# Padding that moves the buffers of the scores and of the first MLP layer, and other unread products around the kernel's work

## The reference, cut to what matters

```
mod = (silu(c) @ wmod)                       # six vectors of 256 per batch: sa, ca, ga, sb, cb, gb
ga, gb = signs kept, magnitudes at least 0.25
h = layernorm(x) * (1 + ca) + sa
scores = (h * w_lhs) @ (h * w_rhs).T          # 1024 x 1024 per batch
x = x + ga * softmax(scores) @ h
h = layernorm(x) * (1 + cb) + sb
x = x + gb * (relu(h @ W1 + b1) @ W2 + b2)    # W1: 256 x 1024, W2: 1024 x 256
```

## The kernel before, in words

| buffer | role | before | mod 512 | changed | mod 512 |
|---|---|---|---|---|---|
| W1hi, W1lo | F stationary | 17024, 25216 | 128 | the same | 128 |
| W2hi, W2lo | G moving | 33408, 41600 | 128 | the same | 128 |
| Phi, Plo | AV stationary | 87104, 99392 | 64 | the same | 64 |
| Lhi, Llo | SC stationary | 111680, 119872 | 64 | the same | 64 |
| Rhi, Rlo | SC moving | 128064, 136256 | 64 | 128512, 136704 | 0 |
| V | AV moving | 144448 | 64 | 144960 | 64 |
| hid_hi, hid_lo | G stationary | 198336, 204480 | 192 | 198848, 204992 | 192 |
| h2hi, h2lo | F moving | 210624, 218816 | 192 | 211520, 219712 | 64 |

## Time and profile before

### The profile page before, as it was taken

How to read it: one execution, slowest core, us unless ns; L and a number is a source line. 1 busy time by engine, 2 the same in 40 slices (tenths; PEclk the granted TensorE clock), 3 DMA queues, 4 the chain that set the end, 5 groups by cost and what they waited for, 6 DMA issues and landing times.

```text
span 691.5 us, 13488 instructions
## 1 busy us (share of the span) xinstructions
PE 686.1 (99%) x4621; PEld 627.7 (91%) x4621; DVE 558.4 (81%) x1059; ACT 427.5 (62%) x625; POOL 361.7 (52%) x396
## 2 busy tenths in 40 slices
PE   9999999999999999999999999999999999999998
PEld 8688899998999989998999989999899998999997
DVE  5699989799898898978989799887989887876421
ACT  3265398736786367683786647864678634845562
POOL 3572576636654386352872458643665434523644
PEclk9999999999999999999999999999999999999999
DMA  8211761137431382315622266112843126003300
GB/s 294 81 49 59 204 193 55 39 107 252 123 100 56 103 232 91 99 61 179 180 67 90 67 226 185 61 38 98 258 121 99 46 91 221 1 1 100 100 31 30
DMA packets 61663, 77.54 MB, mean 112 GB/s; under 512 B 5632, under 2 KB 54336, under 8 KB 61632
## 3 DMA queue, kind: packets, MB, share of 16 engines
q1 hardware_dynamic: 61632, 77.14, 35.5%
HBM read 46.15 MB, written 30.97 MB: 112 GB/s over the span
## 4 chain that ended last, share of the span: by engine, by line
PE 94%; DVE 4%; issue 0%; ACT 0%; DMA 0%; DVEq 0%; ACTq 0%; SPq 0%
PE col L595 9%; PE col L594 9%; PE col L593 9%; PE acc L530 8%; PE acc L531 8%; PE acc L536 8%; PE score L694 8%; PE score L690 8%; PE score L691 8%; PE score L578 4%; PE score L579 4%; PE score L580 4%; PE score L576 2%; PE score L584 2%; PE score L499 1%; DVE S L879 1%
## 5 line engine op out<-in xcount | busy, mean ns | idle before, releaser
L1088 POOL TENSOR_TENSOR hid_lo<-hid,hid_hi 128x512 fp32r<-128x512 f32 x127 | 175.4, 1386 | 143.2 <-ACT hid_hi L719 142.8
L715 ACT ACTIVATE hid<-col,b1T 128x512 f32<-128x512 f32 x128 | 87.0, 679 | 140.3 <-PE col L595 126.1
L530 PE MATMUL acc<-W2hi,hid_hi 128*128 128x256 f32 x480 | 119.2, 282 | 0.0
L531 PE MATMUL acc<-W2lo,hid_hi 128*128 128x256 f32 x480 | 116.9, 278 | 0.0
L690 PE MATMUL score<-V,Phi 128*128 128x258 f32 x448 | 108.8, 281 | 0.0
L691 PE MATMUL score<-V,Phi 128*128 128x256 f32 x448 | 108.6, 281 | 0.0
L719 ACT ACTIVATE hid_hi<-hid 128x512 fp32r<-128x512 f32 x128 | 81.0, 633 | 37.6 <-PE acc L536 29.8
L593 PE MATMUL col<-h2hi,W1hi 128*128 128x512 f32 x256 | 102.4, 400 | 0.0
L595 PE MATMUL col<-h2hi,W1lo 128*128 128x512 f32 x256 | 101.0, 395 | 0.0
L594 PE MATMUL col<-h2lo,W1hi 128*128 128x512 f32 x256 | 100.6, 393 | 0.0
L530 PEld LDWEIGHTS acc<-W2hi,hid_hi 128*128 128x128 f32 x480 | 90.4, 188 | 2.1
(11 more groups left out here) (139 smaller groups left out, 1493.2 us busy)
## 6 DMA issues: line engine op xcount, KB each, us to landing
block_rows<-blocks SPq DMA_DIRECT2D x29, 512.0 KB, 2.9
blocks<-block_rows SPq DMA_DIRECT2D x116, 128.0 KB, 3.0
x_cur<-x SPq DMA_DIRECT2D x16, 512.0 KB, 3.9
ln_t<-x SPq DMA_DIRECT2D x14, 512.0 KB, 4.8
score_blocks<-stage SPq DMA_DIRECT2D x14, 512.0 KB, 4.2
lower<-score_blocks SPq DMA_DIRECT2D x56, 128.0 KB, 2.9
out<-x_mlp SPq DMA_DIRECT2D x8, 512.0 KB, 3.0
out<-x_mlp SPq DMA_DIRECT2D x15, 256.0 KB, 2.2
```

The costliest lines, as they stand in the source:

```text
L530: nc.tensor.matmul(o, hi, W2hi[:, it, :], start=(it == 0 and (apart or t % 2 == 0)), stop=False, skip_group_check=True)
L531: nc.tensor.matmul(o, hi, W2lo[:, it, :], start=False, stop=False, skip_group_check=True)
L715: nc.scalar.activation(hid[:, n % 2, :], col[n % 2][:], ACT.Relu, bias=b1T[:, n % FT:n % FT + 1]).then_inc(col_read, 1)
L1088: G.tensor_tensor(hid_lo[:, n % RING, :], hid[:, n % 2, :], hid_hi[:, n % RING, :].bitcast(F32), ALU.subtract).then_inc(hid_lo_done, 1)
```

## The change

```diff
         Lhi, Llo = sb("Lhi", [P, DK, ROWS], F32R), sb("Llo", [P, DK, ROWS], F32R)
+        sb("before_R", [P, 112])
         Rhi, Rlo = sb("Rhi", [P, DK, ROWS], F32R), sb("Rlo", [P, DK, ROWS], F32R)
+        sb("behind_R", [P, 16])
...
         hid_hi, hid_lo = sb("hid_hi", [P, RING, HR], F32R), sb("hid_lo", [P, RING, HR], F32R)
+        sb("before_h2", [P, 96])
         h2hi, h2lo = sb("h2hi", [P, DK, ROWS], F32R), sb("h2lo", [P, DK, ROWS], F32R)
...
+            def keep_busy_split(moving, stationary, count):
+
+                for _ in range(count):
+                    nc.tensor.matmul(col[0][:, 0:moving.shape[-1]], stationary, moving, start=True, stop=True)
...
                             last.then_inc(tile_done, 1)
+
+                        for at in (120, 96, 32):
+                            keep_busy_split(h2hi[:, 0, 0:HR], W1hi[:, 0, at:at + P], 5)
                     elif kind == "MA":
                         pe.wait_ge(pool_const, 2)
-                        keep_busy(20)
+                        keep_busy(10)
+                        pe.wait_ge(const_ready, 3)
+
+                        keep_busy_split(h2hi[:, 0, 0:1].broadcast_to([P, HR]), h2hi[:, 0, HR:HR + P], 5)
+                        keep_busy_split(h2hi[:, 0, 0:HR], h2hi[:, 0, HR + 32:HR + 32 + P], 5)
                         pe.wait_ge(silu_step, 1)
...
             V_.memset(V_first[:, :, D + 1:VW], 0.0).then_inc(const_ready, 1)
+            V_.memset(h2hi[:, 0, :].bitcast(F32), 0.0).then_inc(const_ready, 1)
```

## The result

The changed kernel takes 695.49 us (median of 8 runs, 694.61 to 695.78), the kernel before 693.53 us on the same chip (8 runs). The ratio is 1.0024, with a 95% interval of 1.0015 to 1.0033: slower, by little more than such a measurement resolves. The forecast was 688.2 us.

A forecast was written before the change was run, and what follows sets the result against it. TensorE was taken as the bound, with products in flight 686.1 of 691.5 us. Savings 4.0 + 2.1 + 1.2 - 1.0 = 6.3, less 0.4 and the end's 0.3, gave 5.6 us: 693.8 to 688.2, range 686.8 to 692.0.

The forecast's parts named there:

- Is 64 as good at 512 columns? One place says so: Last score product ahead of F, at distance 64, lasts 388 ns against its line's mean of 391; taken as evidence for 64.
- a floor for every distance, 388: Shortest duration in ns of 512-column products, used to price F and the wide scores at distance 64.
- F at 448 with 388 and 394 in turn: Warning in the prediction: behind G, F at distance 448 lasts 388 ns on line 593 but 394 on line 595.
- 398 behind AV: Warning in the prediction: F on line 593 lasts 398 ns behind AV, so delay depends on what went before.
- the third, slower: Rival: at 512 columns 64 leads into the 398 ns step everywhere; F +3.8 us, wide scores +1.3, 697.9 us; chance 0.08.
- a weight load that ends halfway: Slower rival's reason: at 512 columns the weight load, about as long as 256 columns, ends halfway; chance 0.08.
- F at 64: F's 768 products, lines 593 to 595, at 388 ns each apart from start-ups: 4.0 us saved.
- Scores: Score products moved to distance 64: 0.8 us saved at 512 columns, 1.0 at 256, 0.3 at 384; together 2.1.
- G behind F: 46 G blocks behind F enter out of step, 0.026 us each; 1.2 us saved if F leaves no such trace.
- Start and end: Start: 20 identity products replaced by ten of 512 columns, nil; end: fifteen unread products finish last, +0.3 us.
- rival 2: Distance does nothing; differences come from the kind of work, PSUM or semaphores; only the end counts, 694.1 us; chance 0.10.

The follow-up runs named there:

- the map: Bare kernels without the kernel's work: TensorE alone runs 24 equal products per operand distance, one operand's place fixed; paces from start to start, no ratio given.
- e7: Kernel before with V's tiles 2304 bytes apart and halves 1024, so AV has distance 64 in every tile; ratio 1.0003 (0.9994 to 1.0012).
- the pairs: Bare kernel without the kernel's work: twelve 512-column products at varying distance, then always the same twelve of 256 columns at 64; no ratio given.

## Why the prediction was wrong

**The step that failed** is "Is 64 as good at 512 columns? One place says so". It isn't: the map has 233 ns at 64 against 229 at 448, where F had stood, and the forecast was 226. The place that I read, the last score product ahead of F with 388 ns, was a single product: in a run at one distance the first products wander (229, 236, 231, 236 at 64; 236, 224, 231, 236, 228, 232, 231, 227 at 0) before they settle, and any one of them can show 388 or 398. What I called a floor for every distance, 388, is the shortest value that wandering or a step with three beats (226, 229, 232 at 448) touches. The trace of the kernel before could have told me. Some score blocks have twelve wide products; in the one that starts at 232.84 us the sixth, behind which the scores go on at a distance of 0, lasts 389 ns, like the sixth and last of the block ahead of F with its 388:

```profile
L580 PE MATMUL score<-Rhi,Llo 128*128 128x512 f32 x1 | 0.4, 389 | 0.0
```

So the 388 belonged to the sixth product of a block at distance 0, and said nothing of 64. I had other signs in hand: F at 448 with 388 and 394 in turn, and 398 behind AV.

**The rival that came true** is the third, slower: at 512 columns 64 leads into a bad step everywhere. That 64 leads into a slow step at 512 columns held, and its size was off; its reason, a weight load that ends halfway, no run tested. It gave +3.8 us to F from a mean of 398 ns; measured were 394 to 395 ns and +1.4 us. It gave +1.3 to the wide scores, measured +0.6, and -1.3 to the narrow ones, measured -0.3.

**F at 64**, forecast -4.0 us: +1.4. **Scores**, forecast -2.1: +0.3 altogether. They had stood at 0, in the maps one of the best distances for 512 columns; their mean was above the floor because 28 of the 35 blocks have only six wide products in a row, and settling takes five to eight. **G behind F**, forecast -1.2: right in kind, 1.04 to 0.49 us, half the size: behind F at 64, G is in the fast step after two or three products where it had mostly taken three to five, but not at once. **Start and end**, forecast 0 and +0.3: the end was +0.35, and of the start's 0.25 I can't say what belongs to the change, since it moves by more than that from one execution to the next. The start did settle one thing: the memset is hidden. **The wait** of AV for `V`, 0.5 us, had no term; it stands in the traces with the unread products, and in e7, at the same place, so it can come up without the unread products too. Its cause I didn't follow.

**The rule that speaks against the change.** The Trainium skill, "TensorE: Matmul & The Clock Gate", section "Step-by-step: what each phase is for", gives the two operands independent read ports. The same Trainium skill, "SBUF — State Buffer", section "A bandwidth-pool intuition that's wrong", knows contention only as structural. By both the distance would do nothing. The runs don't agree: equal products take 113 or 120 ns from start to start at 256 columns by their distance, and 113 or 118 by what ran before them. That the distance does nothing (rival 2, 694.1) came closer in time than my forecast, for a wrong reason: gains and losses of opposite sign.

What stays open: why there are two steps. The weight load of the next product starts with the current product, within 0.01 us in the kernel's timeline; that the two reads disturb each other and that a repeating pattern of delays comes of it is a reading that fits all runs, but no run shows a single delayed read, and none left the weight loads out. Nor is it shown in the kernel what would lead G into the fast step behind an F at 0. In the pairs none of the settings that leave G fast has F at 227 to 229; F at 448 with G at 64, the kernel before, is the best pairing that the runs found, and no variant was faster than it.

## What to carry to other kernels

Where operand placement moves TensorE's pace, it does so for a sequence of products, not for one: measure the settled pace of each width by itself over a few dozen equal products, and then the pairs of stages that follow each other, before shifting a buffer. A placement that is best for one width can be the worst for another. A shortest duration found somewhere in a trace is no floor until a run of products stays there.

## What the runs showed of the hardware

- Products of float32r with a weight load each, at the granted clock of 1.0 (2.4 GHz): 113.2 to 113.6 ns from start to start at 256 columns at best, 226.6 at 512, 173.3 at 384, and 118.7 at 258.
- The pace moves with the addresses of both operands, and in the maps it repeats when one of them moves by 256 bytes: up to 6% at 256 columns (113.6 to 120.4), 3% at 512 (226.6 to 234.7), 2% at 384 (173.3 to 177.3).
- The same twelve products settle at 113.4 or at 117.8 ns, by what ran ahead of them, and stay there. So a value of the maps belongs to its order and its place too: at 512 columns the distance 16 has 227 and 233 ns in the two maps and about 237 in the pairs, the distance 144 has 233 and 231 in the maps and about 227 in the pairs.
- In the changed kernel's start, four of the five products whose moving operand is one column repeated 512 times have distances of 218 to 220 ns, the fifth, at the front, 299; the next ones, with 512 different columns, 230 to 245.
